# A two-layer cross-attention and feed-forward kernel: split products in the first feed-forward layer, and the last batch's queries and keys kept on the chip

## What is computed

```python
x = x + map_attention(LN(x), ctx)      # softmax(q k^T) of the context, applied to x
h = LN(x)                              # token choice: 64 rows of each batch
sel = h[top_k(h @ w_router, 64)]       # 256 rows in all
a = sel + attention(rms(sel)) @ wo     # 16 heads of 128
m = silu(rms(a) @ w_gate) * (rms(a) @ w_up) @ w_down     # inner width 2048
x = x + h with rows idx replaced by gate*(a + m) + (1-gate)*sel
q = head_norm(LN(x) @ Wq + bq); k, v likewise from ctx   # 16 heads of 32
x = x + (softmax(q k^T over 496 keys) v + softmax(over the last 16 keys) v) @ Wo + bo
s = sigmoid(LN(x) @ gate_w)            # 2 of 4 groups, then 6 of 32 experts
x = x + sum_6 weight * expert(LN(x)) + shared(LN(x))     # inner 352, shared 704
```

## Time and profile before

| | |
|---|---|
| median of 3 runs | 2324.6 us (2318.51 to 2326.18) |
| the profiled execution | 2321.27 us, of it 2319.5 us from first to last instruction |
| mean granted TensorE clock | 0.927 |
| busy | PE 86%, DVE 50%, POOL 48%, ACT 24% |

### The profile page before, as it was taken

One profiled execution on the slowest core, in us unless ns is written; L12 is line 12 of the kernel. 1 busy time (PEld: TensorE's weight loads), 2 busy tenths in 40 slices (PEclk: granted clock), 3 DMA queues, 4 the chain that ended last, 5 costly groups with the idle time before them and its releaser, 6 DMA issues. The chain is left out here.

```text
span 2319.5 us, 33400 instructions
## 1 busy us (share of the span) xinstructions
PE 1985.2 (86%) x10468; PEld 1420.9 (61%) x10469; DVE 1158.2 (50%) x2208; ACT 550.7 (24%) x1158; POOL 1114.0 (48%) x552
## 2 busy tenths in 40 slices
PE   5946886987881788999889999999999999998992
PEld 3423443433330333333379999999999999987882
DVE  2564442046674566776665435445444444556331
ACT  3220222101111444454222222121212212111110
POOL 0000000002553455655215558767766868879886
PEclk8977997998995689999999999999999999998996
DMA  3042001402115337651014544544544555555999
GB/s 115 0 132 82 18 27 73 154 0 102 73 73 181 103 122 238 206 171 42 13 61 169 188 155 148 183 157 149 181 164 144 167 169 179 178 168 156 205 212 216
DMA packets 199486, 305.96 MB, mean 132 GB/s; under 512 B 16473, under 2 KB 94809, under 8 KB 199417
## 3 DMA queue, kind: packets, MB, share of 16 engines
q1 hardware_dynamic: 141624, 187.24, 25.4%
q0 software_dynamic: 21504, 50.93, 9.4%
q10 hardware_dynamic: 36288, 66.84, 8.2%
HBM read 186.42 MB, written 118.55 MB: 131 GB/s over the span
## 5 line engine op out<-in xcount | busy, mean ns | idle before, releaser
L2253 PE MATMUL psum<-e_gu_high,e_rowT_high 128*128 (+1 forms) x1272 | 429.0, 339 | 6.6 <-issue 4.0
L2253 PE MATMUL psum<-e_gu_low,e_rowT_high 128*128 (+1 forms) x1272 | 409.2, 324 | 0.0
L1977 ACT ACTIVATE e_silu<-psum 128x352 f32<-128x352 f32 x159 | 73.9, 465 | 870.4 <-PE psum L2258 808.9
L2253 PEld LDWEIGHTS psum<-e_gu_high,e_rowT_high 128*128 128x128 f32 x1272 | 241.0, 189 | 33.5 <-issue 29.2
L2258 PE MATMUL psum<-e_gu_high,e_rowT_low 128*128 (+1 forms) x1272 | 255.3, 323 | 0.0
L2253 PEld LDWEIGHTS psum<-e_gu_low,e_rowT_high 128*128 128x128 f32 x1272 | 241.8, 190 | 3.5
L2055 DVE TENSOR_TENSOR e_midT_low<-psum,e_midT_high 128x256 fp32r<-128x256 f32 x159 | 67.5, 424 | 319.5 <-ACT e_midT_high L1986 297.9
L2258 PEld LDWEIGHTS psum<-e_gu_high,e_rowT_low 128*128 128x128 f32 x1272 | 213.5, 189 | 0.0
L2273 PE MATMUL psum<-e_d_high,e_midT_high 128*128 (+3 forms) x477 | 187.8, 394 | 1.0 <-ACT e_midT_high L1986 1.0
L2273 PE MATMUL psum<-e_d_low,e_midT_high 128*128 (+3 forms) x477 | 188.3, 395 | 0.0
L1906 POOL TENSOR_TENSOR e_gu_high<-f_gu_in,e_ones 128x1408 fp32r<-128x1408 f32 x31 | 79.8, 2573 | 183.6 <-PE psum L2258 175.2
(11 more groups left out here) (348 smaller groups left out, 3763.0 us busy)
## 6 DMA issues: line engine op xcount, KB each, us to landing
d_sorted<-f_hs SPq DMA_DIRECT2D x32, 1048.0 KB, 9.5
e_row<-d_sorted ACTq DMA_DIRECT2D x125, 262.0 KB
d_y<-f_arena ACTq DMA_DIRECT2D x127, 256.0 KB
f_gu_in<-in_L_ffn_w_gate SPq DMA_DIRECT2D x32, 704.0 KB, 5.2
f_gu_in<-in_L_ffn_w_up SPq DMA_DIRECT2D x32, 704.0 KB, 5.1
f_d_in<-in_L_ffn_w_down SPq DMA_DIRECT2D x32, 512.0 KB
d_y<-f_hs SPq DMA_DIRECT2D x8, 1024.0 KB, 5.7
f_d_in<-in_L_ffn_w_down SPq DMA_DIRECT2D x32, 192.0 KB
```

The lines of the kernel that those rows point to most:

```text
L2253: nc.tensor.matmul(bank[:, 0:M].unsqueeze(1), rowT_high[par][:, k, :], w[:, bass.ds(buffer, 1), k, at:at + M], start=(k == 0 and n == 0), ...
```

## The change

1. The feed-forward of the chosen rows works as the routed layer does. Weights come in 12 pieces of 1 MB through four raw buffers; ACT rounds each to `high`, DVE subtracts to get `low`, in rings of four; a product is three sets of 8 matmuls, one instruction each, in place of 8 float32 matmuls. Pieces 0 and 1 are loaded during the attention before.
2. A class `Scores` holds what groups 0 and 1 need. Their row loads, turns and splits, and the maxima of group 0, move into the last batch of project_heads, and the maxima from n = 3 alternate between two pairs of banks. The rows of groups 2 and 3 are loaded there too.
3. The last batch's q and k are not finished in project_heads, but stay in memory (in the places of `mixed_odd` and of `w_o`): q lacks scale, weight and bias, k the squares too. In context_attention ACT squares k in group 0, DVE sums, POOL raises to -1/2, DVE finishes q in group 1 and k in group 2, between `scale_values(g-1, 1)` and maximum 6. In its turn for group 3 SP stores both, waits for k's landing, loads the output weights into its place, waits for q's, and goes on with the rows of group 5.
4. In project_heads the copy `ctx_b` goes, and the output bias is added after `finish` of q.
5. In the routed layer the two memsets of `rank_members` move to the start and the rest behind `shared_steps(2)`; POOL waits, after each of the three early groups of three gathers, until the last has landed.

```diff
+            def load_piece(sp, p): ...   # raw[p % RAW], RAW = RING = 4, EARLY = 2
...
+                    if h == 2:
+                        for p in range(EARLY):
+                            load_piece(sp, p)
...
+                for p in range(EARLY, len(PIECES)):
+                    if p >= RAW:
+                        sp.wait_ge(piece_low, p - RAW + 1)
+                    load_piece(sp, p)
...
+                low_of(0, 1)
+                rms_dve(dve)
+                dve.wait_ge(hT_high_ready, 1)
+                nc.vector.tensor_tensor(hT_low[:], hT[:], hT_high[:].bitcast(F32), ALU.subtract).then_inc(hT_low_ready, 1)
+                low_of(2, 3)
+                multiply(0)
...
+                high_of(0, 1)
+                rms_act(act)
+                act.wait_ge(hT_written, 1)
+                nc.scalar.copy(hT_high[:], hT[:]).then_inc(hT_high_ready, 1)
+                high_of(2, 3)
+                silus(0)
...
+                def product(at, p):
+                    pe.wait_ge(piece_low, p + 1)
+                    for g in range(GROUPS):
+                        for k in range(CC):
+                            for m, w in enumerate((high, low)):
+                                nc.tensor.matmul(c.bank[at + g][:], hT_high[:, k, rows], w[p % RING][:, k, :], ...)
+                    pe.wait_ge(hT_low_ready, 1)
+                    for g in range(GROUPS):
+                        for k in range(CC):
+                            last = nc.tensor.matmul(c.bank[at + g][:], hT_low[:, k, rows], high[p % RING][:, k, :], ...)
```

```diff
 project_heads, last batch
+                    if j == JT - 1 and b == B - 1:
+                        early.find_max(dve, 0, 0)
+                        add_bias(b)
+                        early.find_max(dve, 0, 1)
...
+                if b < B - 1:
+                    sum_squares(b, 1)
+                    finish(b, 0, q[par][:], q_scaled)
+                    add_bias(b)
+                    finish(b, 1, k[par][:], k_scaled)
+            for n in range(2, early.PAIRS):
+                early.find_max(dve, 0, n)
...
+            for n in range(2, early.PAIRS):
+                if n == 3:
+                    pe.wait_ge(k_copied, B * JT - 1)
+                early.scores(pe, 0, n)
+                if n < 4:
+                    pe.wait_ge(early.exact_ready[3 - n], n - 1)
+                    early.turn_rows(pe, 1, n - 2)
```

```diff
 context_attention
+                if g == GPB - 1:
+                    for ready, name, tile, landed in ((q_scaled, "d_xq", mixedT[1], q_stored), (k_scaled, "d_xk", w_o, k_stored)):
+                        sp.wait_ge(ready, 1)
+                        sp.dma_start(c.dram[name][B - 1].rearrange("(j p) d -> p j d", p=P), tile[:]).then_inc(landed, 16)
+                    sp.wait_ge(k_stored, 16)
+                    sp.dma_start(w_o[:], c.dram["L1_xattn_Wo"].rearrange("(k p) n -> p k n", p=P)).then_inc(w_loaded, 16)
+                    sp.wait_ge(q_stored, 16)
...
+                if g == 0:
+                    dve.wait_ge(k_squared, 1)
+                    of = early.hrstd[:, 1, :]
+                    chain.link(nc.vector.reduce_sum(of, squares.rearrange("p h (n d) -> p (h n) d", d=HD), AX.X))
+                    nc.vector.tensor_scalar(of, of, 1.0 / HD, 1e-6, ALU.mult, ALU.add).then_inc(k_var_ready, 1)
+                if g == 1:
+                    chain.link(early.scale_heads(0, mixedT[1][:]))
+                    chain.link(early.affine_heads(0, 0, mixedT[1][:]))
+                    early.affine_heads(0, 1, mixedT[1][:]).then_inc(q_scaled, 1)
+                if g == 2:
+                    dve.wait_ge(k_rstd_ready, 1)
+                    chain.link(early.scale_heads(1, w_o[:]))
+                    chain.link(early.affine_heads(1, 0, w_o[:]))
+                    early.affine_heads(1, 1, w_o[:]).then_inc(k_scaled, 1)
```

```diff
 routed_ffn
                 if e < E_ - 1:
-                    gather(range(BETWEEN * (e - E_ + 4), BETWEEN * (e - E_ + 5)))
+                    last = gather(range(BETWEEN * (e - E_ + 4), BETWEEN * (e - E_ + 5)))
+                    pool.wait_ge(gathered[last % GATHERS], 16 * (last // GATHERS + 1))
...
-            rank_members()
             shared_steps(2)
+            rank_members()
             lay_out_tiles()
```

More of the change, by code:

```diff
@@ L765, in _, with low_of, multiply @@
             def _(dve):
-                rms_dve(dve)
-                with dve.Fori(0, PARTS) as n:
+                def low_of(*pieces):
+                    for p in pieces:
+                        dve.wait_ge(piece_high, p + 1)
+                        nc.vector.tensor_tensor(low[p % RING][:], raw[p % RAW][:], high[p % RING][:].bitcast(F32), ALU.subtract).then_inc(piece_low, 1)
+                def multiply(n):
                     dve.wait_ge(silu_ready, n + 1)
@@ L831, in _ @@
[L831 to L842 removed]
+                            for m, w in enumerate((high, low)):
+                                nc.tensor.matmul(c.bank[6 + g][:], midT_high[:, g, k * P:(k + 1) * P], w[p % RING][:, k, :],
+                                                 start=(n == 0 and k == 0 and m == 0), stop=False)
@@ new lines, in down @@
+                    pe.wait_ge(midT_low_ready, n + 1)
+                    for g in range(GROUPS):
+                        for k in range(4):
+                            last = nc.tensor.matmul(c.bank[6 + g][:], midT_low[:, g, k * P:(k + 1) * P], high[p % RING][:, k, :],
+                                                    start=False, stop=(n == PARTS - 1 and k == 3))
+                    return last
+                for p, (kind, n) in enumerate(PIECES):
+                    if kind == "gate":
+                        if n >= 1:
+                            pe.wait_ge(silu_ready, n)
+                        product(0, p).then_inc(gated, 1)
+                    elif kind == "up":
+                        if n >= 1:
+                            turn_mid(n - 1)
+                        product(2, p).then_inc(upped, 1)
+                    else:
+                        if n == PARTS - 1:
+                            turn_mid(n)
+                        down(n, p).then_inc(out_ready, 1)
@@ L1079, in _ @@
                     for a in range(2):
+                        if b == B - 1 and j == JT - 1:
+                            early.scores(pe, 0, a)
                         bank = by_head(c.bank[2 * (j % 2) + a])
@@ L1239, in context_attention @@
         ones = sbuf(nc, stack, "y_ones", [P, 2, HD])
-        gu_flat = c.gu_in[:].rearrange("p k n -> p (k n)")
-        row = [gu_flat[:, n * 2 * S:(n + 1) * 2 * S].rearrange("p (a j d) -> p a j d", a=2, j=JT) for n in range(2)]
-        exact = [gu_flat[:, 4 * S:5 * S], c.d_in[:, 0, :]]
-        high = [sbuf(nc, stack, f"y_{a}_high", [P, 3, S], F32R) for a in KINDS]
-        low = [sbuf(nc, stack, f"y_{a}_low", [P, 3, S], F32R) for a in KINDS]
+        high, low, sel = early.high, early.low, early.sel
         v = sbuf(nc, stack, "y_v", [P, 2, JT, P])
@@ L1950, in gather @@
                                                  compute_op=ALU.add).then_inc(gathered[n % GATHERS], 16)
+                return n
             with pool.Fori(2, E_ // 2 - 1) as n:
```

450 lines of the change are left out of this document (271 added, 179 removed).

## The result

The changed kernel takes 2290.4 us in the median of 4 runs (2286.43 to 2295.12), the one before 2324.3 beside it (2318.51 to 2326.18): 0.9863 of the time, 95% interval 0.9844 to 0.9881. The forecast was 2288, the range 2269 to 2304. The profiled execution of the changed kernel is the longest of its four, 2295.1 us with a span of 2293.4; the two profiled executions thus lie 26.2 apart, the medians 33.9. What follows splits the 26.1 us of the two spans, always with one mark of the trace to the next.

What follows compares the result with a forecast made beforehand. PE was taken as the rule (39% of the chain), with gains where it idles, and POOL's list as setting the end. Terms -12.5 - 51.3 + 23.5 - 1.9 + 7.5 = -34.7 from 2321.3 gave 2286.6, put at 2288; range 2269 to 2304.

Steps and rivals of the forecast that it cites:

- part 1: Feed-forward of the chosen rows with split operands: -12.5 us, bounds -16 (no late start, 0.233 us an instruction) and +2.2.
- part 5: Early gathers in the routed layer: three landing waits make the last split later, +7.5 us, bounds 0 and +14.
- Feed-forward, -12.5: Feed-forward of the chosen rows: 288 instructions at 0.235 us save 14.7 us, a later start costs 2.2.
- rival (b): Feed-forward gets no faster because a ring slot, rounding or piece comes late each time: 2300 us, chance 0.11.
- Seam, -51.3: Between head projections and context attention: PE's idle stretch goes, maxima cost 1.3 us each; -51.3 us, bounds -53 and -46.
- Context attention, +23.5: Finishing q and k there costs +1.8, +10.1, +10.1, +1.5 us in groups 0 to 3; bounds +13 and +32.
- (a): Context attention, groups 1 and 2: POOL does not hold DVE's new instructions, they run at once; 2278 us, chance 0.20.
- (c): Context attention: DVE's new two-operand instructions are held through a row of POOL's, up to 11.85 us each; 2358 us, chance 0.04.
- Ranking, -1.9: Routed layer's ranking: PE's 2.68 us idle in shared tile 2 shrinks to two short subtracts; -1.9 us (0 to -2.7).
- Landing waits, +7.5: Early gathers: each group's last gather taken to land 5.1 us after its start, making POOL's last split 7.3 us later.
- rival (d): Early gathers: the end hangs on PE, so lost DVE stalls come off and waits add nothing; 2257 us, chance 0.03.
- part 4: Ranking in the routed layer: scan moved into DVE's wait for PE's counts, memsets into ACT's first rounding; -1.9 us.

Runs made afterwards that it cites:

- e5: The changed kernel with the six steps finishing q and k spread singly over groups 0 to 3, SP storing k after its other loads: 2271.4 us (0.9777).
- e3: The changed kernel with one-operand multiplications by 1 replacing scale, weight and bias of the last batch's q and k: 2281.4 us (0.9832).
- e2: The kernel before the change with only the three landing waits added: 2336.6 us (1.0064).
- e11: The changed kernel with the ranking's scan and two memsets back ahead of DVE's steps for shared tile 2: 2294.8 us (0.9877).
- e1: The changed kernel with the three landing waits taken out: 2274.0 us (0.9800).

## Why the prediction was right, and where it was not

The time was forecast within 2.4 us of the median. Part of that is luck: against the profiled executions the sum of -34.7 missed by 8.6, and the median lay 4.7 below the profiled one. Two terms were 6.3 and 7.3 us too small, and the total stayed inside the range all the same. Two of the sums don't come out as written: the bound of -16 in part 1 is -15.3 (288 x 0.233 from 82.4), and part 5 adds up to 7.6; neither changes the forecast.

- *Feed-forward, -12.5, came as -13.0,* with an attention that ended 1.1 us later; without that it is -14.1. The size that was off is 0.227 us an instruction and not 0.235 (288 of them, 2.3 us less). The start was 2.5 us late for 2.2. The lower clock of the first instructions, which I had left out, costs 2.0 us, but the kernel before pays 1.7 there too, so it adds only 0.3. Loads, roundings and low parts were all in time; rival (b) falls.
- *Seam, -51.3, came as -51.6*, with 697.2 for the turn where 698 was named.
- *Context attention, +23.5, came as +22.5.* By groups +1.8, +9.6, +9.8, +1.4, -1.7, +1.6 against +1.8, +10.1, +10.1, +1.5. Holding, its lengths and its order were as told; e5 shows the price was that of a place, and e3 that the rule behind it is wider than I used it. By the rule of the Trainium skill (SBUF — State Buffer, section "Who interferes with whom") the two groups cost 20.2, without it 9.8, and they cost 19.4, or 16.9 against the turns of e2; 9.6 of that is holding that the rows show. Rivals (a) and (c) fall, (c) because `mix` ends the row of POOL's instructions.
- *Ranking, -1.9, came as -3.8* (e11). I had said where scan and memsets go, but priced only PE's wait and not the 3.7 us by which DVE's list gets shorter up to the first slots.
- *Landing waits, +7.5, came as +13.8*, shown by e1 and e2. This is the mis-sized term. I took a gather as landed when few of its packets were left in the earlier trace rows, 5.1 us after its start. POOL goes on 6.6, 6.9 and 8.2 us after it: 21.8 where I had 15.3, the 6.5 us that are missing. The mechanism, POOL's list at the end, was right, and rival (d) falls.
- *Not forecast, +7.3, of which 1.3 came back up to the first early gather:* the first routed tile behind the scatters, 4.7 us of it the later row and 2.5 the lower clock behind the wait. It was in the trace of before: PE arrived there without a wait, but the chain of 172.1 us ended only just ahead of it. In the changed kernel the row is there 5.8 us after the last scatter's issue; so counted it was ready 0.9 us before PE came in the kernel before (1380.9 + 5.8 against 1387.6), an estimate. I gave the gain of part 4 to a path without asking what stands beside it.

## What to carry to other kernels

Work that leaves a stage between two others doesn't vanish; its price is that of the place where it is put, and here the same six steps cost 19 us more in one place of two groups than spread over places where their engine waits and its neighbour is idle. Read a DMA's landing from what starts behind it, not from where its packets thin out. Before a gain is carried through to the end, look for chains that arrive with PE at the same place without a wait in the trace; they take the gain, and their scatter hides the next one.

## What the runs showed of the hardware

- DVE, with two operands from the memory, and POOL hold each other for whole instructions, in the order in which they begin: 3.87 us behind an add of 4.51, and POOL's 1.27 turned into 3.31. Instructions of DVE with one operand that went through 2048 columns in 1.23 us were held too, a sum over 2048 columns in 2.28 was not.
- In a split that follows POOL's gathers at once, its instructions overlap by 0.6 us in the records, and DVE's two-operand instructions got no turn for 9.8 and 11.4 us; with the last landing awaited first, neither happened. Why the landing matters is open.
- Four scatters in flight in POOL's queue: PE stood for 99 of 131 us, ACT and DVE with it, 107 us in the total; why is argued, not shown. Three in flight: no stop, and 4.7 us less than with two (the intervals of the two ratios just overlap).
